# The first fp32 sums of down's adapter set one product later, and the next network's first weights scaled ahead of the low rows of t

## The chip, the cores and the metric

The kernel runs on one core of a Trainium2 chip. The metric is the time of one execution on the device, in microseconds (us); each kernel was run several times, and the median is given. Beside that there is one profiled execution of the kernel before. Its instruction records are the trace.

Five engines work side by side, each through its own list of instructions in order: TensorE (PE; its weight loads are PEld), VectorE (DVE), ScalarE (ACT), GpSimd (POOL) and SyncE (SP, which here only starts transfers). They hand work to one another by semaphores: an instruction raises a count when it is done, and another engine's list stands still at a wait until the count is reached.

## The reference, cut to what matters

The input x holds 8 samples of 128 tokens with 512 features, 1024 tokens in all. Two layers are added to it. In each, a first network is conditioned per sample by low-rank adapters that an index picks, and a feed-forward network stands behind it.

```python
# layer 0, first network (F = 1376, 16 adapters of rank 16)
gate = x @ W_gate.T + 0.5 * (x @ A_gate[id].T) @ B_gate[id].T
up   = x @ W_up.T   + 0.5 * (x @ A_up[id].T)   @ B_up[id].T
act  = silu(gate) * up
down = act @ W_down.T + 0.5 * (act @ A_down[id].T) @ B_down[id].T
# layer 0, second network (I = 1792): each weight is w * (su @ sv), rank 4
d    = silu(down @ gate_eff.T) * (down @ up_eff.T)
x    = x + d @ down_eff.T
# layer 1: a 512x512 product with bias and adapters, then a network of
# group-scaled integer weights (I = 1792)
x    = x + int_ffn(cond1(x))
```

The change touches two places in the first half: the sums `act @ A_down[id].T` (called t here) of the first network, and the step in which the first tile of the second network's weights is multiplied with its rank-4 scale.

## The kernel before

Tokens lie along the free axis, in two chunks `c` of 512; features lie on the 128 partitions. A product of fp32 accuracy is made of three passes of the PE with operands split into a high and a low part: high x high, high x low, low x high. The high part is a copy by ACT, the low part a subtraction by DVE (`lo`, line 1295). So every weight tile goes through one ACT and one DVE instruction before the PE uses it, and so does every result that is multiplied again.

The work before the integer network is a list of phases: "cond gate/up a", "cond down a", "cond gate/up b", "cond down b", "ffn0 gate/up a", and so on. A gate/up phase runs over tiles of 128 hidden features. For each tile the PE makes four products in this order (`gate_up_tile`, line 1902): gate of chunk 0, up of chunk 0, gate of chunk 1, up of chunk 1. Each is 12 matmuls and 2 adapter matmuls (line 1848). ACT then takes the silu (984), DVE multiplies with up (1395), ACT and DVE make the high and the low part (994, 1295). The first two tiles of the first phase are done together, so that all their results come at once; the third tile is the first of the ordinary kind.

The sums t of down's adapter are made along the way, in fp32, out of the fp32 product `gated`. `t_down` (2106) takes one hidden tile: 8 records of a matmul with 32 columns, summed in the bank `ps_m`, and it first waits until that tile's and its neighbour's products are made (`prod_done`) and until the adapters are in order (`a_dn_ready`). It is called for two tiles at a time, inside the third and the fifth tile of a gate/up phase, behind the gate product of chunk 0. `gated` is reused every second tile, so ACT's next silu into it waits for `t_read`, which `t_down` raises.

In "cond down b" the order around the change is written out by hand. In step o = 0 the PE makes the scale of the second network's first weight tile in the bank `ps_gates` (`scales`, 1880), half of the first down product, the last `t_down`, and the other half. DVE then masks and halves t (line 1673), makes its low part in 8 small pieces (`lo_of_t_down`, 1341), and calls `first_weights` (1537): it waits for the weights' transfer (`first_raw_in`) and for the scale (`m_ready`), multiplies the two (1542, raises `w_prod`), and goes on with three block sums and two low parts of the weights. In step o = 1 the PE starts with the scale of the second weight tile in `ps_m`. It waits for t to be masked, because that scale overwrites `ps_m`, and for `w_prod` to reach 1:

```python
if ph.name == "cond down b" and 2 * i + jj == 1:
    pe.wait_ge(t_masked, CH + 1)
    scales(following[ph], 0, 1)      # waits for w_prod >= 1
```

Behind that stand the next down product (12 to 15 matmuls a chunk) and `down_adapters` (2084), which needs the high and the low rows of t (`t_hi_rows`, `t_lo_rows_done`).

Of the kernel before, what the change touches and what calls it, by code (L numbers as in the profile page):

```python
# [61 lines left out]
def plan_phases():  # L62
    steps = [
        ("cond gate/up a", "gate_up", "cond", 0, CUT, 0, 1, "split"),
        ("cond down a", "down", "cond", 0, HK, 0, 1, "split"),
        ("cond gate/up b", "gate_up", "cond", 1, NKD - CUT, CUT, 1, "split"),
        ("cond down b", "down", "cond", 1, HK, CUT, 2, "split"),
        ("ffn0 gate/up a", "gate_up", "ffn0", 0, 7, 0, 1, "scale"),
        ("ffn0 down a", "down", "ffn0", 0, HK, 0, 1, "scale"),
        ("ffn0 gate/up b", "gate_up", "ffn0", 1, 7, 7, 1, "scale"),  # L70
        ("ffn0 down b", "down", "ffn0", 1, HK, 7, 1, "scale"),
        ("cond1", "down", "cond1", 0, HK, 0, 1, "split"),
    ]

    t0, s0, g0, d0 = 0, 0, 0, 0
    phases = []
    for name, kind, layer, part, tiles, first, loads, prep in steps:
        s0 += name == "ffn0 gate/up a"
        phases.append(Phase(name, kind, layer, part, tiles, first, t0, s0, g0, d0, loads, prep))
        t0 += tiles  # L80
        s0 += tiles
        if kind == "gate_up":
            g0 += CH * tiles
        else:
            d0 += CH * tiles
    return phases
# [78 lines left out]
def adaln_ffn(nc, d, out):  # L165
    phases = plan_phases()
# [6 lines left out]
    with ExitStack() as ctx:  # L173
# [176 lines left out]
        def chunk(c):  # L350
            return slice(c * CT, (c + 1) * CT)
# [4 lines left out]
        def widths(ph, i, jj):  # L356

            if ph.layer == "cond" and ph.part == 1 and isinstance(i, int) and 2 * i + jj == ph.tiles - 1:
                return F0_TAIL
            return P  # L360
# [11 lines left out]
        def slot(ph, jj, i):  # L372

            return (ph.s0 + jj) % 2
# [38 lines left out]
        def pair_tokens(pair):  # L413
            return slice(pair * PT, (pair + 1) * PT)
# [3 lines left out]
        def pair_sums(c):  # L418
            return slice(c * CT, c * CT + PT)
# [7 lines left out]
        def quarter(n):  # L427
            return slice(n * PR, (n + 1) * PR)
# [856 lines left out]
        def _(dve):  # L1285
# [8 lines left out]
            def lo(out_, value, hi):  # L1294
                return nc.vector.tensor_tensor(out_, value, hi.bitcast(F32), ALU.subtract)  # L1295
# [36 lines left out]
            def lo_of_t(c, nets):  # L1332
                dve.wait_ge(t_hi_done, (0 if nets == 2 else CH + 1) + c + 1)
                for g in range(nets):
                    for half in range(2):
                        rows = quarter(2 * g + half)
                        for row in (2, 3) if nets == 1 else (2,):
                            last = lo(t_rows[quarter(row), g, pair_tokens(2 * c + half)], gated[rows, c, 0:PT], t_hi[rows, c, 0:PT])
                last.then_inc(t_lo_rows_done, 1)

            def lo_of_t_down():

                dve.wait_ge(t_hi_done, CH + 1)
                for c in range(CH):
                    for pair in (2 * c, 2 * c + 1):
                        for row in (2, 3):
                            last = lo(t_rows[quarter(row), 0, pair_tokens(pair)], gated[quarter(pair), 0, 0:PT], t_hi[quarter(pair), 0, 0:PT])
                    last.then_inc(t_lo_rows_done, 1)
# [166 lines left out]
            def piece_lo(ph, j, piece):  # L1515

                q, cols = tile_of(ph, j), pieces[piece]
                if piece == 2:
                    dve.wait_ge(w_hi_done, ph.t0 + j)
                else:  # L1520
                    dve.wait_ge(piece_hi_done, 2 * q + piece + 1)
                value = w7_total[j % 2][:, cols] if piece else raw_weights(ph, j)[:, 2 * P:6 * P]
                lo(w7_lo[j % 2][:, cols], value, w7_hi[j % 2][:, cols]).then_inc(w_ready if piece == 2 else piece_ready, 1)

            def block_sums(ph, j, part):

                raw, low = raw_weights(ph, j), w7_total[j % 2]
                half = raw.rearrange("p (r h n) -> p r h n", r=2, h=2)
                if part == 0:
                    nc.vector.tensor_tensor(low[:, pieces[1]].rearrange("p (r n) -> p r n", r=2), half[:, :, 0],  # L1530
                                            half[:, 0:1, 1].to_broadcast([P, 2, 2 * P]), ALU.add).then_inc(w_summed, 1)
                elif part == 1:
                    nc.vector.tensor_tensor(low[:, 12 * P:14 * P], raw[:, 4 * P:6 * P], raw[:, 6 * P:8 * P], ALU.add).then_inc(w_summed, 1)
                else:
                    nc.vector.tensor_tensor(low[:, 8 * P:12 * P], raw[:, 0:4 * P], raw[:, 4 * P:8 * P], ALU.subtract).then_inc(w_summed, 1)

            def first_weights(ph):

                dve.wait_ge(first_raw_in, 16)
                dve.wait_ge(m_ready, 1)  # L1540
                raw = w_raw_first[:, :]
                nc.vector.tensor_tensor(raw, raw, ps_gates[:, :], ALU.mult).then_inc(w_prod, 1)
                dve.wait_ge(w_prod, 1)
                for part in range(3):
                    block_sums(ph, 0, part)
                for piece in range(2):
                    piece_lo(ph, 0, piece)
# [121 lines left out]
            def small_t(ph):  # L1669

                if ph.name == "cond down b":
                    dve.wait_ge(t_read, NKD)
                    nc.vector.scalar_tensor_tensor(out=gated[:, 0, 0:PT], in0=ps_m[:, 0:PT], scalar=0.5, in1=seg_mask[:, :],
                                                   op0=ALU.mult, op1=ALU.mult).then_inc(t_masked, 1)
                    lo_of_t_down()
                    first_weights(named["ffn0 gate/up a"])
                    return
                for c in range(CH):
                    here = gated[0:RB, c, 0:PT]
                    dve.wait_ge(t_lo_rows, c + 1)  # L1680
                    nc.vector.scalar_tensor_tensor(out=here, in0=ps_m[0:RB, pair_sums(c)], scalar=2.0, in1=here, op0=ALU.mult, op1=ALU.add).then_inc(t_added, 1)
                    dve.wait_ge(t_added, c + 1)
                    nc.vector.tensor_tensor(here, here, seg_mask[0:RB, :], ALU.mult).then_inc(t_masked, 1)
                for c in range(CH):
                    lo_of_t(c, 1)

            nc.vector.memset(warm[:, :].bitcast(F32), 0.0).then_inc(warm_zero, 1)
            for n, item in enumerate(start):
# [4 lines left out]
                else:  # L1693
                    _, c, k = item
# [13 lines left out]
            for ph in phases:  # L1708
# [33 lines left out]
                def adapters_step(ph, o):  # L1742

                    nxt = following.get(ph)
                    if o == 0:
                        tile_lo(ph, 0, 1)
                        small_t(ph)
# [82 lines left out]
        def _(pe):  # L1830
# [71 lines left out]
            def gate_up_tile(ph, i, jj):  # L1902
                s, m = slot(ph, jj, i), widths(ph, i, jj)
                pe.wait_ge(w_ready, ph.t0 + 2 * i + jj)
                for c in range(CH):
                    n = ph.g0 + CH * (2 * i + jj) + c
                    for g, (ps, read, ready) in enumerate(((ps_gate, silu_done, gate_ready), (ps_up, prod_done, up_ready))):
                        if not isinstance(i, int) or n >= CH:

                            pe.wait_ge(read, n - 3 if ph is phases[0] and 2 * i + jj == 2 else n - 1)  # L1910

                        def input_ready(k, c=c, g=g):

                            if g == 0 and ph.name == "ffn0 gate/up a" and jj == 0 and isinstance(i, int) and i == 0:
                                pe.wait_ge(h_ready, CH * k + c + 1)

                        last = sums(ps[c], m, s, g * HK * P, range(HK), lambda k, r, c=c: h_hi[0:r, k, chunk(c)],
                                    lambda k, r, c=c: h_lo[0:r, k, chunk(c)], before=input_ready, stop=ph.layer != "cond")
                        if ph.layer == "cond":
                            last = gate_up_adapters(ps[c], m, ph, 2 * i + jj, g, c)  # L1920
                        last.then_inc(ready, 1)
                        if g == 0 and c == 0 and 2 * i + jj in (2, 4):
                            for j in (2 * i + jj - 2, 2 * i + jj - 1):
                                t_down(ph, j)

# [349 lines left out]
```

## Time and profile before

| | us |
|---|---|
| median of 3 runs | 640.12 (639.88 to 640.39) |
| the profiled execution's own time | 636.58 |
| its span, first to last instruction | 635.0 |
| PE busy | 620.7 |
| DVE busy | 449.1 |
| ACT busy | 315.3 |
| POOL busy | 245.1 |

The mean granted clock of TensorE is 0.999 of full speed. A row of the page's or the trace's answers has the start, the duration, the engine, the line of the kernel, the operation with what it writes and reads, and in brackets how long the engine had been idle and who ended that. Matmuls are pipelined, so their durations overlap; what counts is when the next one starts.

### The profile page before, as it was taken

The numbers are of one execution on the slowest core, as the hardware profiler recorded it, in microseconds if no ns is written. First come the engines' busy times: TensorE is split into PE (matmuls) and PEld (weight loads), VectorE is DVE, ScalarE is ACT, GpSimd is POOL, SyncE is SP. The second block draws the span as 40 slices with busy tenths as digits, with TensorE's granted clock in tenths as the row PEclk, the third lists the DMA queues.
The fourth block names the chain that finished last, engine by engine and source line by source line (L and its number), as shares of the span: only waits on it lengthen the run. The fifth ranks groups of instructions, "written<-read, shape, count | busy, mean of one in ns | idle before, by whom it ended". The sixth has DMA issues, their size and how long they took to land.

```text
span 635.0 us, 8094 instructions
## 1 busy us (share of the span) xinstructions
PE 620.7 (98%) x2964; PEld 497.1 (78%) x2964; DVE 449.1 (71%) x540; ACT 315.3 (50%) x418; POOL 245.1 (39%) x197
## 2 busy tenths in 40 slices
PE   8989999999998999999999999999999999999996
PEld 6768788788777876778787787878787888788885
DVE  4475454544457998885437888735678998999987
ACT  5664525344634344443113444425557887478860
POOL 3670010000000006752023656440003898959986
PEclk9999999999999999999999999999999999999999
DMA  8750022101021111321102100152213211212203
GB/s 254 177 149 26 26 85 87 57 13 44 21 73 51 49 34 59 140 59 59 33 34 99 34 33 30 61 112 52 93 67 101 62 59 62 101 66 69 82 0 133
DMA packets 24474, 45.19 MB, mean 71 GB/s; under 512 B 9972, under 2 KB 12020, under 8 KB 24372
## 3 DMA queue, kind: packets, MB, share of 16 engines
q1 hardware_dynamic: 21972, 40.80, 20.9%
q0 software_dynamic: 2176, 3.36, 2.0%
q8 instruction: 24, 0.39, 0.2%
q10 hardware_dynamic: 288, 0.52, 0.2%
q14 instruction: 14, 0.11, 0.1%
HBM read 40.74 MB, written 2.10 MB: 67 GB/s over the span
## 4 chain that ended last, share of the span: by engine, by line
PE 83%; DVE 6%; ACT 3%; issue 3%; POOL 1%; SPq 1%; DMA 1%; DVEq 0%
PE ps_down L1838 7%; PE ps_down L1839 7%; PE ps_down L1840 7%; PE ps_up L1838 4%; PE ps_up L1839 4%; PE ps_up L1840 4%; PE ps_m L2020 3%; PE ps_m L2021 3%; PE ps_up L2020 3%; PE ps_gate L2020 3%; PE ps_down L2020 3%; PE ps_down L2021 3%; PE ps_gate L2021 3%; PE ps_up L2021 3%; PE ps_gate L1838 2%
## 5 line engine op out<-in xcount | busy, mean ns | idle before, releaser
L813 POOL TENSOR_TENSOR act_lo<-up,act_hi 128x512 fp32r<-128x512 f32 x14 | 18.2, 1298 | 195.7 <-ACT act_hi L1086 195.7
L1838 PE MATMUL ps_down<-act_hi,w_hi 128*128 128x512 f32 (+1 forms) x180 | 71.2, 396 | 0.0
L1839 PE MATMUL ps_down<-act_lo,w_hi 128*128 128x512 f32 (+1 forms) x180 | 70.3, 391 | 0.0
L1840 PE MATMUL ps_down<-act_hi,w_lo 128*128 128x512 f32 (+1 forms) x180 | 70.1, 389 | 0.0
L844 POOL TENSOR_TENSOR up_sum<-up_sum,up_more 128x1024 f32<-128x1024 f32 x14 | 33.7, 2410 | 64.4 <-DVE up_more L1411 64.4
L1295 DVE TENSOR_TENSOR w_lo<-w_raw,w_hi 128x512 fp32r<-128x512 f32 (+4 forms) x41 | 44.4, 1083 | 18.1 <-ACT w_hi L915 13.4
L915 ACT ACTIVATE w_hi<-w_raw 128x1024 fp32r<-128x1024 f32 (+4 forms) x30 | 27.0, 900 | 45.9 <-DVE w_raw L1302 22.0
L1838 PEld LDWEIGHTS ps_down<-act_hi,w_hi 128*128 128x128 f32 (+1 forms) x180 | 33.8, 188 | 7.8 <-issue 0.4
L1840 PEld LDWEIGHTS ps_down<-act_hi,w_lo 128*128 128x128 f32 (+1 forms) x180 | 33.8, 188 | 7.2
L1839 PEld LDWEIGHTS ps_down<-act_lo,w_hi 128*128 128x128 f32 (+1 forms) x180 | 33.8, 188 | 6.6
L1295 DVE TENSOR_TENSOR b_rows<-b_raw,b_hi 32x1024 fp32r<-32x1024 f32 (+2 forms) x23 | 25.4, 1104 | 19.2 <-ACT b_rows L933 12.0
L1411 DVE SCALAR_TENSOR_TENSOR gate_sum<-ps_up,s_group,gate_sum 128x1024 f32<-128x1024 f32 x28 | 35.8, 1280 | 4.0 <-PE ps_up L2021 4.0
L856 POOL TENSOR_TENSOR act_lo<-gate_sum,act_hi 128x1024 fp32r<-128x1024 f32 x14 | 38.3, 2747 | 0.0
L1838 PE MATMUL ps_up<-h_hi,w_hi 128*128 128x512 f32 (+1 forms) x96 | 38.0, 396 | 0.0
L1839 PE MATMUL ps_up<-h_lo,w_hi 128*128 128x512 f32 (+1 forms) x96 | 37.6, 392 | 0.0
L1840 PE MATMUL ps_up<-h_hi,w_lo 128*128 128x512 f32 (+1 forms) x96 | 37.4, 389 | 0.0
L1658 DVE TENSOR_TENSOR xp<-xp,ps_down 128x512 f32<-128x512 f32 x20 | 13.6, 684 | 31.6 <-PE ps_down L1840 30.5
L1080 ACT ACTIVATE w_hi<-w_total 128x512 fp32r<-128x512 f32 (+1 forms) x28 | 20.7, 739 | 30.6 <-POOL w_total L807 18.3
L1295 DVE TENSOR_TENSOR w_lo<-w_total,w_hi 128x512 fp32r<-128x512 f32 (+1 forms) x28 | 27.6, 986 | 10.8 <-ACT w_hi L1080 10.7
L1965 PE MATMUL ps_gate<-x_hi,w_hi 128*128 128x512 f32 x80 | 31.9, 398 | 1.0 <-ACT m_copy L1066 0.9
L1838 PE MATMUL ps_gate<-h_hi,w_hi 128*128 128x512 f32 (+1 forms) x80 | 31.6, 395 | 0.3 <-DVE h_lo L1295 0.3
L1839 PE MATMUL ps_gate<-h_lo,w_hi 128*128 128x512 f32 (+1 forms) x80 | 31.4, 392 | 0.0
(295 smaller groups left out, 1784.1 us busy)
## 6 DMA issues: line engine op xcount, KB each, us to landing
w_int<-in_ffn_gu SPq DMA_DIRECT2D x14, 512.0 KB, 3.5
w_raw<-in_cond_gu SPq DMA_DIRECT2D x9, 512.0 KB, 3.4
w_raw<-in_ffn_gu SPq DMA_DIRECT2D x9, 512.0 KB, 3.6
w_raw<-in_ffn_dn SPq DMA_DIRECT2D x8, 448.0 KB, 3.3
w_int<-in_ffn_dn SPq DMA_DIRECT2D x8, 448.0 KB, 3.2
xp<-in_x SPq DMA_DIRECT2D x8, 256.0 KB, 5.3
w_raw_third<-in_ffn_gu SPq DMA_DIRECT2D x4, 512.0 KB, 3.5
xp<-in_x SPq DMA_DIRECT2D x1, 2048.0 KB, 9.4
```

Source lines behind the costliest of these rows:

```text
L844: nc.gpsimd.tensor_tensor(up_sum[:, u % 3, :], up_sum[:, u % 3, :], up_more[:, u % 2, :], ALU.add).then_inc(up_done, 1)
L856: nc.gpsimd.tensor_tensor(act_lo[:, j, :], gate_sum[:, u % 4, :], act_hi[:, j, :].bitcast(F32), ALU.subtract).then_inc(unit_ready, 1)
L915: nc.scalar.activation(w_hi[:, s, n], w_raw[:, s, n], ACT.Copy).then_inc(w_hi_done, 1)
L1080: nc.scalar.activation(w7_hi[j % 2][:, pieces[piece]], value, ACT.Copy).then_inc(done, 1)
L1295: return nc.vector.tensor_tensor(out_, value, hi.bitcast(F32), ALU.subtract)
L1411: return nc.vector.scalar_tensor_tensor(out=here, in0=group_bank(g), scalar=group_scale(g), in1=here, op0=ALU.mult, op1=ALU.add)
L1838: nc.tensor.matmul(ps[0:m, :], w_hi[0:r, s, cols], rhs_hi(k, r), start=start and n == 0, stop=False)
L1839: nc.tensor.matmul(ps[0:m, :], w_hi[0:r, s, cols], rhs_lo(k, r), start=False, stop=False)
L1840: last = nc.tensor.matmul(ps[0:m, :], w_lo[0:r, s, cols], rhs_hi(k, r), start=False, stop=stop and n == len(ks) - 1)
L1965: nc.tensor.matmul(banks[n][:, :], w7_hi[s][:, cols], x_hi[n][:, k, :], start=not more and k == 0, stop=False, skip_group_check=more)
L2020: nc.tensor.matmul(bank[:, chunk(c)], weights, hi[:, chunk(c)], start=True, stop=False)
L2021: last = nc.tensor.matmul(bank[:, chunk(c)], weights, lo[:, chunk(c)], start=False, stop=True)
```

## The change

It does two things. In the third tile of the first phase the two calls of `t_down` move from behind the gate product of chunk 0 to behind the up product of chunk 0. In the other places (the fifth tile, and both places of "cond gate/up b") they stay. And `first_weights` is cut in two: its wait for the transfer and the scale and its product become `first_product`, which DVE calls between the masking of t and `lo_of_t_down`.

```diff
-            def first_weights(ph):
+            def first_product():
 
                 dve.wait_ge(first_raw_in, 16)
                 dve.wait_ge(m_ready, 1)
                 raw = w_raw_first[:, :]
                 nc.vector.tensor_tensor(raw, raw, ps_gates[:, :], ALU.mult).then_inc(w_prod, 1)
+
+            def first_weights(ph):
+
                 dve.wait_ge(w_prod, 1)
                 for part in range(3):
                     block_sums(ph, 0, part)
...
                     nc.vector.scalar_tensor_tensor(out=gated[:, 0, 0:PT], in0=ps_m[:, 0:PT], scalar=0.5, in1=seg_mask[:, :],
                                                    op0=ALU.mult, op1=ALU.mult).then_inc(t_masked, 1)
+                    first_product()
                     lo_of_t_down()
                     first_weights(named["ffn0 gate/up a"])
...
-                        if g == 0 and c == 0 and 2 * i + jj in (2, 4):
+                        if c == 0 and (g, 2 * i + jj) in ((int(ph is phases[0]), 2), (0, 4)):
                             for j in (2 * i + jj - 2, 2 * i + jj - 1):
                                 t_down(ph, j)
```

On the PE, in the third tile, the order before is this. `ps_gate` and `ps_up` are the gate and up sums of the chunk, `gated` and `gated_odd` the products of the first and the second tile; the 9 matmuls left out are of the same up product.

```order
L1848 MATMUL ps_gate<-t_rows,b_rows 128x256 x2
L2113 MATMUL ps_m<-gated,a_dn 32x256 x4
L2113 MATMUL ps_m<-gated_odd_58,a_dn 32x256 x4
L1838 MATMUL ps_up<-h_hi,w_hi 128x512
L1839 MATMUL ps_up<-h_lo,w_hi 128x512
...
L1848 MATMUL ps_up<-t_rows,b_rows 128x256 x2
L1838 MATMUL ps_gate<-h_hi,w_hi 128x512
```

With the change (whose lines are 4 further down in this part of the file) the same place reads:

```order
L1852 MATMUL ps_gate<-t_rows,b_rows 128x256 x2
L1842 MATMUL ps_up<-h_hi,w_hi 128x512
L1843 MATMUL ps_up<-h_lo,w_hi 128x512
...
L1852 MATMUL ps_up<-t_rows,b_rows 128x256 x2
L2117 MATMUL ps_m<-gated,a_dn 32x256 x4
L2117 MATMUL ps_m<-gated_odd_58,a_dn 32x256 x4
L1842 MATMUL ps_gate<-h_hi,w_hi 128x512
```

The two groups over `a_dn` stand behind the up product's 14 matmuls and ahead of the gate product of chunk 1.

On DVE, in step o = 0 of "cond down b", the difference is the following. `seg_mask` is the mask of t, `t_rows` the low rows of t, `w_raw_first` the second network's first weights.

```order
 L1295 TENSOR_TENSOR w_lo<-w_raw,w_hi 128x640
-L1673 SCALAR_TENSOR_TENSOR gated<-ps_m,seg_mask 128x256
+L1676 SCALAR_TENSOR_TENSOR gated<-ps_m,seg_mask 128x256
+L1542 TENSOR_TENSOR w_raw_first<-w_raw_first,ps_gate 128x1024
 L1295 TENSOR_TENSOR t_rows<-gated,t_hi 32x256 x8
-L1542 TENSOR_TENSOR w_raw_first<-w_raw_first,ps_gate 128x1024
 L1530 TENSOR_TENSOR w_total_97<-w_raw_first 128x512
 L1533 TENSOR_TENSOR w_total_97<-w_raw_first 128x256
```

The product of 1024 columns moved ahead of the eight low parts; the block sums stay behind them. ACT's and SP's lists, and POOL's, are as they were.

## Rows read from the trace of the kernel before

**Rows 1.** The page: the span, and the granted clock in 40 slices.
```profile
span 635.0 us, 8094 instructions
...
PEclk9999999999999999999999999999999999999999
```

**Rows 2.** The waits of PE over the whole span, longest first.
```profile
engine line waited for: us in total, times, longest us
PE ps_m L1880 <- DVE w_raw_first L1542: 2.2, 1, 2.2
PE ps_m L2113 <- DVE gated_odd L1395: 2.0, 1, 2.0
...
PE ps_gate L1965 <- ACT m_copy L1066: 0.9, 1, 0.9
```

**Rows 3.** Busy time of each engine in stretches, with PE's granted clock.
```profile
core 0: us, PE busy (x) PEld busy (x) DVE busy (x) ACT busy (x) POOL busy (x), PEclk, DMA share, GB/s
...
192.00:195.00 3.00, 0.81 (x10) 0.57 (x9) 2.91 (x6) 1.44 (x3) 0.00 (x0) 1.00 0.00 0
...
220.00:245.00 25.00, 24.02 (x108) 18.73 (x107) 24.14 (x39) 12.45 (x22) 4.04 (x3) 1.00 0.14 51
```

**Rows 4.** PE in order of time, third to fifth tile: start, us, line.
```profile
38.11 0.40 PE L1848 MATMUL ps_gate<-t_rows,b_rows 128*128 128x256 f32 x2
...
40.55 0.64 PE L2113 MATMUL ps_m<-gated,a_dn 128*32 128x256 f32 x8 [2.04 <-DVE gated_odd L1395]
...
41.55 0.50 PE L1838 MATMUL ps_up<-h_hi,w_hi 128*128 128x512 f32 x1
...
44.40 0.40 PE L1848 MATMUL ps_up<-t_rows,b_rows 128*128 128x256 f32 x2
...
62.51 0.40 PE L1838 MATMUL ps_gate<-h_hi,w_hi 128*128 128x512 f32 x1
```

**Rows 5.** DVE and ACT in order of time, beside the third tile.
```profile
39.73 0.67 DVE L1395 TENSOR_TENSOR gated_odd<-gated_odd,ps_m 128x512 f32<-128x512 f32 x1
...
44.30 0.60 ACT L984 ACTIVATE gated<-ps_gate 128x512 f32<-128x512 f32 x1
...
59.10 1.23 DVE L1295 TENSOR_TENSOR w_lo<-w_raw,w_hi 128x1024 fp32r<-128x1024 f32 x1
```

**Rows 6.** PE in order of time, "cond down b", from step 0 into step 1.
```profile
191.81 0.39 PE L1840 MATMUL ps_down<-act_hi,w_lo 96*128 96x512 f32 x1
...
194.39 0.66 PE L1880 MATMUL ps_m<-pack_long,pack_short 32*128 32x128 f32 x8 [2.19 <-DVE w_raw_first L1542]
...
198.53 0.63 PE L1848 MATMUL ps_down<-t_rows,b_down 128*128 128x256 f32 x4
```

**Rows 7.** DVE in order of time, "cond down b".
```profile
188.62 0.42 DVE L1673 SCALAR_TENSOR_TENSOR gated<-ps_m,seg_mask 128x256 f32<-128x256 f32 x1 [1.94 <-PE ps_m L2113]
189.53 3.46 DVE L1295 TENSOR_TENSOR t_rows<-gated,t_hi 32x256 fp32r<-32x256 f32 x8 [0.48 <-ACT t_hi L952]
193.02 1.22 DVE L1542 TENSOR_TENSOR w_raw_first<-w_raw_first,ps_gate 128x1024 f32<-128x1024 f32 x1
...
197.03 0.82 DVE L1295 TENSOR_TENSOR w_lo<-w_raw,w_hi 128x640 fp32r<-128x640 f32 x1
...
201.36 1.22 DVE L1302 TENSOR_TENSOR w_raw<-w_raw,ps_m 128x1024 f32<-128x1024 f32 x1 [1.11 <-DMA w_raw<-in_ffn_gu]
203.40 0.82 DVE L1295 TENSOR_TENSOR w_lo<-w_raw,w_hi 128x640 fp32r<-128x640 f32 x1 [0.81 <-ACT w_hi L915]
...
214.15 0.69 DVE L1658 TENSOR_TENSOR xp<-xp,ps_up 128x512 f32<-128x512 f32 x1 [0.60 <-PE ps_up L1848]
...
220.38 1.29 DVE L1295 TENSOR_TENSOR x_lo<-x_total,x_hi 128x512 fp32r<-128x512 f32 x2 [0.29 <-ACT x_hi L1061]
```

**Rows 8.** The first weights' transfer: when it was issued, and us to landing.
```profile
183.82 0.34 SPq L731 DMA_DIRECT2D w_raw_first<-in_ffn_gu  x1
...
w_raw_first<-in_ffn_gu SPq DMA_DIRECT2D x1, 512.0 KB, 3.5
```

## The prediction, made before the changed kernel ran

> **What bounds the kernel.** The views were read in this order. The page first: over a span of 635.0 us the granted clock is at its full level in every slice [rows 1]. Then PE's waits over the whole span. PE is busy nearly all the time, so an idle stretch of PE is a candidate for time that can come off the end, and only two of those waits are longer than a microsecond and a half in the middle of the kernel: 2.2 us of the scale product L1880 on DVE's product of the first weights, and 2.0 us of the fp32 sums L2113 on DVE's product of the second tile [rows 2]. The change moves one instruction group at each of them. Then the order of time around each, on the engine that waits and on those it waits for [rows 4 to 8].
>
> **First part: the fp32 sums one product later.** What is there: the two adapter matmuls of gate, chunk 0, start at 38.11 us; PE then stands for 2.04 us, until DVE's product of the second tile is done at 39.73 + 0.67 = 40.40 us, and the sums start at 40.55 [rows 4, 5]. They take until 41.55, 1.00 us, and then comes up, chunk 0, whose adapter matmuls start at 44.40; with their 0.12 us spacing the product fills 41.55 to about 44.63, 3.08 us.
> With the change, up starts right behind the gate product: 40.55 - 2.04 = 38.51 us. It ends at 38.51 + 3.08 = 41.59. The sums come next, and what they wait for has been there since 40.40, so 1.2 us of cover are left. They take their 1.00 us as before, on the path both times. Gate, chunk 1, starts at 42.6 in place of 44.6. **Term: -2.04 us.** Nothing is added and nothing else changes its place.
> What could be late next: the silu of this tile's gate, chunk 0, waits for the sums to have read the old `gated`. They end at 42.6 at the latest, and ACT comes to it only at 44.30, since it is busy with adapter pieces until then [rows 5]; 1.7 us of cover. That silu does not move with PE. PE writes its bank next in the fourth tile, three products of 3.08 us and the sums behind 38.5, at about 48.7, 3.8 us after the silu's end, so it does not hold PE either; were the cover gone, those 3.8 us would be the next. The fifth tile is the nearest thing with less room: its low weights are made at 59.10 to 60.33 and PE starts on it at 62.51 [rows 4, 5], 2.2 us of room against 2.04 gained. Even if DVE did not move at all there, PE would just not wait; and DVE and ACT are released there by results of the third tile's last product, which come 2 us earlier too.
>
> **Second part: the weights' product ahead of t's low parts.** What is there: PE's last matmul of step 0 starts at 191.81 and leaves the engine free at 192.20; the scale product starts at 194.39, 2.19 us idle. It waited for DVE, whose order was mask (188.62, 0.42), wait for ACT's high part (0.48), eight low parts (189.53, 3.46), product (193.02, 1.22, done 194.24) [rows 6, 7]. Of the 3.0 us from 192 to 195 PE was busy for 0.81 [rows 3].
> With the change the product stands behind the mask. Its operands: the scale is made in step 0, before the first down product; the transfer was issued at 183.82 and took 3.5 us, so it is there by 187.4 [rows 8], 1.6 us before DVE asks. The product runs 189.05 to 190.27 and PE, which comes at 192.20, finds it done, with 1.9 us of cover. The other condition, t masked, is met at 189.04. **Term: -2.19 us** at this place.
> What is behind the moved product on DVE: the eight low parts start at 190.27 in place of 189.53 (the 0.48 us wait for ACT now falls behind the product and is gone), and end at 193.73. PE needs them for the adapters, at 198.53 before and 198.53 - 2.19 = 196.34 now: 2.6 us of room. The block sums start at about 193.7, where they started behind 194.24; DVE is 0.5 to 0.7 us early from there on, not 2.19. This is the place where the gain can get lost.
> So I follow DVE further. Its low weights at 197.03 come some 0.6 us early; their end releases the transfer on which L1302 at 201.36 waited 1.11 us, and so that too comes 0.6 early, at 200.8, and ends at 202.0. The next low weights, at 203.40, had waited 0.81 us for ACT, and ACT for PE; with PE 2.19 us early they start when L1302 is done, at 202.0: 1.4 us early. At 214.15 DVE had waited 0.60 us for PE: it starts at 214.15 - 0.60 - 1.4 = 212.1, PE's result being there at 211.96, so 2.0 us early. At 220.38 another 0.29 us of waiting for an x part, which ACT makes behind a copy of a PE result, gives the rest: 2.2 us early [rows 7]. From 220 to 245 DVE is busy 24.14 of 25.00 us and PE 24.02 [rows 3]; PE's next wait of note, 0.9 us on `m_copy` [rows 2], lies there and hangs on DVE's chain. By then DVE is as early as PE, so it stays 0.9 and does not grow. Between 196 and 220 PE asks DVE for low weights that are made a tile ahead: those of 197.03 + 0.82 - 0.6 = 197.3 are for step 2, which PE reaches only behind the adapters of 196.3 and another half of step 1, past 200.
> The bounds of this part: 2.19 us if the above holds; 0.6 us if DVE's own lead is all that survives its busy stretch; no wait is added that could turn it below nothing unless the transfer is late (below). I take 2.1 to 2.19, since each idle stretch of DVE that makes up the lag is in the rows.
>
> **The clock.** Every slice, and the 3 us in which PE idled, has a granted clock at the 2.4 GHz level [rows 1, 3]: the two idle stretches did not lower it, so taking them away gives their own length and no more. The Trainium skill, TensorE: Matmul & The Clock Gate, section "What's actually happening", says that throttled is the default state and that activity releases it, so idle time can cost more than its length. The trace disagrees for stretches of 2 us here. It is kept as a rival, since the timed runs are longer than the profiled one.
>
> **Sum.** Span 635.0 - 2.04 - 2.19 = 630.8 us. What lies around it is 636.58 - 635.0 = 1.58, so the profiled execution would read 632.4. The median of the runs is 640.12, 3.5 us above the profiled one; I take the difference off it unchanged: 640.12 - 4.2 = **635.9 us**. A difference of 0.2% (1.3 us) is about what a measurement of this kernel can tell from no change.
>
> **Rivals.**
> *DVE keeps its lag* (0.13). The second gain shrinks because DVE is only 0.6 us early where its queue is full. Against it: DVE's waits of 0.81, 0.60 and 0.29 us on the others [rows 7]; for it: the almost full stretch behind [rows 3]. It gives 640.12 - 2.04 - 0.6 = 637.5, at the mildest 636.5.
> *One of the two waits stands up again on the spot* (0.06), on an operand I take for ready: 640.12 - 2.1 = 638.0.
> *The change does not do what it says* (0.03): both waits are only carried on to the next product, where another count is as late. 640.1. Against it: the covers of 1.2 and 1.9 us.
> *Slower* (0.03). DVE now waits for the weights' transfer with t's low parts queued behind it. If the transfer lands late, 3.46 us of low parts that used to lie beside that wait come behind it, and the block sums, the low weights and all of DVE's full stretch with them. It costs nothing until a landing at 189.0, eats up the second gain from there on, and turns to a loss once the landing is later than 193.0, 5.7 us later than seen; then DVE's chain is up to 3.46 us late: 640.12 - 2.04 + 3.46 = 641.5. For it: SP starts the next down tile's transfers right behind it; against it: 3.5 us to landing [rows 8].
> *More than the stalls* (0.05). The timed runs are 3.5 us longer than the profiled one. If that is TensorE at the 1.2 GHz level behind these two stalls, it goes with them: 640.12 - 4.2 - 3.5 = 632.4. No row shows it. By that section of the skill it could be so.
>
> **How the numbers follow.** Forecast 0.70, rivals 0.13, 0.06, 0.03, 0.03, 0.05. The range goes from the forecast with some 0.7 us of spread below, 635.2, to the case in which one half fails, 638.2; with 0.70, 0.13 and 0.06 less the edges it holds a good 8 in 10. Faster than by 1.3 us, below 638.8: 0.70 + 0.13 + 0.06 + 0.05, taken as 0.93; within: 0.04; slower: 0.03.
>
> **What would show it.** Right: PE's waits no longer have L1880 on the first weights nor the sums on `gated_odd`; the sums start near 41.6 us behind up's adapters; in "cond down b" the scale product starts near 190.2 (192.4 less the 2.04 of the first part) with no idle time ahead; the low rows of t end before PE reaches the adapters; the wait on `m_copy` is still near 0.9 us; span near 630.8. Wrong: new idle time of PE of half a microsecond or more between 194 and 245 us with DVE named, most of all a grown `m_copy` wait (DVE's lag); or idle time of DVE ahead of the product of the first weights on a transfer.

## The result: 7.4 us faster, where 4.2 were forecast

| | us |
|---|---|
| before, median of 4 runs | 640.0 (639.55 to 640.39) |
| changed, median of 4 runs | 632.55 (632.18 to 633.65) |
| ratio | 0.9887, 95% interval 0.987 to 0.9904 |
| profiled execution of before: span, granted clock | 635.0, 0.999 |
| profiled execution of the changed kernel: span, granted clock | 630.5, 1.000 |

The direction was right, and so was the span of the profiled execution (630.8 forecast, 630.5 seen). The median was not: 635.9 forecast, 632.55 measured, below the range of 635.2 to 638.2. So the two profiled executions differ by 4.5 us, about what was forecast, and the medians by 7.4. The question for the experiments is where the other 3 us were.

### The profile after

The page's first line, then PE's waits, longest first; they answer to [rows 1] and [rows 2].

```profile
span 630.5 us, 8094 instructions
```

```profile
engine line waited for: us in total, times, longest us
PE ps_m L2124 <- DVE warm L1691: 1.7, 1, 1.7
PE ps_gate L1969 <- ACT m_copy L1066: 0.9, 1, 0.9
PE ps_m L1902 <- DVE w_raw L1312: 0.7, 1, 0.7
```

Both waits of [rows 2] that the change aims at are gone, and the wait on `m_copy` is still 0.9 us. PE in order of time in the third tile, as [rows 4]: start, us, line.

```profile
37.87 0.40 PE L1852 MATMUL ps_gate<-t_rows,b_rows 128*128 128x256 f32 x2
38.10 0.40 PE L1842 MATMUL ps_up<-h_hi,w_hi 128*128 128x512 f32 x1
...
41.18 0.64 PE L2117 MATMUL ps_m<-gated,a_dn 128*32 128x256 f32 x8
...
42.18 0.50 PE L1842 MATMUL ps_gate<-h_hi,w_hi 128*128 128x512 f32 x1
```

Up follows the gate product without a gap, the sums follow up and have no idle time ahead. From the gate's adapters to the next gate product it is 42.18 - 37.87 = 4.31 us; before it was 44.63 - 38.11 = 6.5 us by [rows 4], 2.2 less. "cond down b": first DVE, as [rows 7], then PE's scale product, as [rows 6].

```profile
186.32 0.42 DVE L1676 SCALAR_TENSOR_TENSOR gated<-ps_m,seg_mask 128x256 f32<-128x256 f32 x1 [1.94 <-PE ps_m L2117]
186.66 1.21 DVE L1542 TENSOR_TENSOR w_raw_first<-w_raw_first,ps_gate 128x1024 f32<-128x1024 f32 x1
187.90 3.46 DVE L1295 TENSOR_TENSOR t_rows<-gated,t_hi 32x256 fp32r<-32x256 f32 x8
191.39 0.69 DVE L1530 TENSOR_TENSOR w_total<-w_raw_first 128x512 f32<-128x512 f32 x1
...
198.62 1.22 DVE L1302 TENSOR_TENSOR w_raw<-w_raw,ps_m 128x1024 f32<-128x1024 f32 x1 [2.47 <-DMA w_raw<-in_ffn_gu]
```

```profile
189.82 0.66 PE L1884 MATMUL ps_m<-pack_long,pack_short 32*128 32x128 f32 x8
...
193.95 0.63 PE L1852 MATMUL ps_down<-t_rows,b_down 128*128 128x256 f32 x4
```

The product is done at 187.87, 1.95 us before PE comes for it. The low rows are done at 191.36, 2.6 us ahead of the adapter matmuls. DVE waits longer for the next weights (2.47 us in place of 1.11): its additions ahead of that wait, which hang on PE's results, start at 194.88 where they started at 198.96, 4.1 us earlier, and the weights came 2.7 us earlier. No wait of PE stems from it.

### The profile page after: what moved, and what is told of

Its sections match the earlier page's. It is cut to its first block, busy times and chain, and to the rows that moved or that the text cites. A ratio compares the mean times of both kernels' runs of the same rounds, so it can differ in the third digit from the quotient of the medians.

```text
span 630.5 us, 8094 instructions
## 1 busy us (share of the span) xinstructions
PE 620.3 (98%) x2964; PEld 496.8 (79%) x2964; DVE 448.9 (71%) x540; ACT 315.3 (50%) x418; POOL 245.4 (39%) x197
## 4 chain that ended last, share of the span: by engine, by line
PE 86%; DVE 5%; ACT 3%; issue 2%; POOL 1%; DMA 1%; SPq 0%; DVEq 0%
PE ps_down L1842 7%; PE ps_down L1843 7%; PE ps_down L1844 7%; PE ps_up L1842 4%; PE ps_up L1843 4%; PE ps_up L1844 4%; PE ps_gate L1842 3%; PE ps_gate L1843 3%; PE ps_m L2024 3%; PE ps_gate L1844 3%; PE ps_m L2025 3%; PE ps_up L2024 3%; PE ps_gate L2024 3%; PE ps_down L2024 3%; PE ps_down L2025 3%; PE ps_gate L2025 3%
```

## The experiments

Each kernel was profiled once and executed several times more beside the kernel before on the same chip. For every execution the span and the mean granted clock over the span are given. That list is what settles the case, so it stands first, as a whole; the kernels in it are described below.

| kernel | executions | median span | at a mean clock of 0.998 or more: count, median span | at 0.997 or less: count, median span |
|---|---|---|---|---|
| before | 68 | 636.9 | 17, 635.2 | 51, 637.5 |
| sums moved alone | 10 | 634.6 | 4, 633.2 | 6, 635.8 |
| product moved alone | 6 | 634.5 | 2, 633.3 | 4, 635.0 |
| changed | 19 | 631.1 | 19, 631.1 | 0 |
| changed, 1 us idle added | 9 | 632.2 | 9, 632.2 | 0 |
| changed, 2 us idle added | 12 | 634.2 | 6, 633.5 | 6, 635.0 |
| changed, 5 us idle added | 12 | 637.4 | 0 | 12, 637.4 |
| sums one product later still | 5 | 630.8 | 5, 630.8 | 0 |
| and adapters ordered later | 5 | 631.2 | 5, 631.2 | 0 |

### Each half alone

The first kernel has only the condition in PE's gate/up tile from the change:

```diff
-                        if g == 0 and c == 0 and 2 * i + jj in (2, 4):
+                        if c == 0 and (g, 2 * i + jj) in ((int(ph is phases[0]), 2), (0, 4)):
```

> Only the fp32 sums of the third tile are moved; the weights' product stays behind the low rows of t. By the sum of the prediction the span falls by 2.04 us, and PE's wait of 2.2 us on the first weights stays. Theory 1 (clock): the kernel before loses 3.2 us more in its timed runs than in its profiled one because TensorE falls to its lower level behind one of the two stalls. Then the timed gain is 2.0 us, or 2.0 + 3.2 = 5.2 us if this stall is the one. Theory 2 (the extra 3.2 us has nothing to do with the stalls): the timed gain over the kernel before on the same chip is 2.0 us here, and 4.2 us, not 7.4, for the whole change when both are timed side by side.

The second has only the product:

```diff
                                                    op0=ALU.mult, op1=ALU.mult).then_inc(t_masked, 1)
+                    first_product()
                     lo_of_t_down()
```

> Only the product of the first weights is moved ahead of the low rows of t; the fp32 sums stay behind gate's chunk 0 and PE waits 2.0 us there. By the sum the span falls by 2.19 us. Theory 1 (clock): the timed gain is 2.2 us, or 2.2 + 3.2 = 5.4 us if the stall in cond down b is the one behind which the clock falls. Theory 2: 2.2 us timed.

Measured: 636.22 and 636.07 us against 638.49 for the kernel before on that chip; ratios 0.9962 (0.9947 to 0.9977) and 0.9952 (0.9936 to 0.9968). The two halves are worth about the same and add up to the whole. Theory 1 in the form in which it was put, that one of the two stalls is the one behind which the clock falls, is wrong: neither half alone brings the 5 us. But the clock is not out of it: with either half alone it is still low in most executions, 6 of 10 and 4 of 6. The profiled execution of the first one is one of these. These are PE, DVE and the others in stretches of 2 us behind the remaining stall, with the granted clock ahead of the last two columns:

```profile
core 0: us, PE busy (x) PEld busy (x) DVE busy (x) ACT busy (x) POOL busy (x), PEclk, DMA share, GB/s
190.00:192.00 2.00, 0.39 (x2) 0.00 (x0) 1.94 (x4) 0.98 (x3) 0.00 (x0) 1.00 0.00 0
192.00:194.00 2.00, 1.42 (x10) 1.28 (x11) 1.97 (x4) 1.44 (x3) 0.00 (x0) 0.82 0.00 0
194.00:196.00 2.00, 2.00 (x6) 1.52 (x6) 2.00 (x4) 0.45 (x1) 0.00 (x0) 0.50 0.00 0
196.00:198.00 2.00, 2.00 (x9) 1.59 (x8) 0.04 (x1) 0.00 (x0) 0.00 (x0) 0.83 0.40 76
```

```profile
192.58 0.66 PE L1880 MATMUL ps_m<-pack_long,pack_short 32*128 32x128 f32 x8 [2.19 <-DVE w_raw_first L1542]
...
194.55 0.63 PE L1838 MATMUL ps_up<-act_hi,w_hi 128*128 128x512 f32 x1
```

The wait is the same 2.19 us as in [rows 6]. Behind it TensorE is at 0.50 of full speed, the 1.2 GHz level, and a matmul record that takes 0.39 us elsewhere takes 0.63. What is lost is 2.0 x (0.18 + 0.50 + 0.17) = 1.7 us. The span of this execution is 634.8 us, and those of the same kernel at a clock of 0.999 are 633.1 to 634.4: 1.7 us above the shortest.

The profiled execution of the second is at a mean clock of 0.996 too, and it shows something else. PE's rows, and the clock at two places:

```profile
11.93 0.50 PE L1842 MATMUL ps_up<-h_hi,w_hi 128*128 128x512 f32 x1 [1.76 <-DVE w_lo L1295]
...
12.97 0.63 PE L1843 MATMUL ps_up<-h_lo,w_hi 128*128 128x512 f32 x1
...
44.03 0.64 PE L2117 MATMUL ps_m<-gated,a_dn 128*32 128x256 f32 x8 [2.07 <-DVE gated_odd L1395]
```

```profile
14.00:16.00 2.00, 2.00 (x7) 1.54 (x6) 0.74 (x2) 1.36 (x3) 1.79 (x5) 0.50 1.22 262
...
44.00:46.00 2.00, 1.97 (x20) 1.34 (x21) 1.27 (x2) 1.96 (x3) 0.00 (x0) 1.00 0.86 242
```

The stall that this kernel keeps, 2.07 us at the sums, did not lower the clock this time. It fell near the start of the kernel instead, behind a wait of 1.76 us for low weights whose transfer was late (ACT had waited 2.09 us for it). So a low mean clock does not prove by itself that one of the two stalls was behind it. In the other twelve traces PE's longest wait in that tile is 1.2 us, and its clock stayed full behind it. None of the 38 executions of kernels with both stalls gone (the changed one, the two with more cover, the one with 1 us added) was at 0.997 or less. So the low clock in most executions goes with the two stalls, and a fall at such a third place is rare.

### Before and changed once more

> The kernel before, timed against itself, with the granted clock and the span of each run. Theory 1 (clock): most runs read about 640 us with a granted clock visibly below that of the profiled run (0.999), and some read 636.6 with a clock near 1. Theory 2: the clock is the same in the long and the short runs, and the extra time is elsewhere. Ratio 1.000 either way, give or take 0.2%.

> The changed kernel, timed side by side with the kernel before on the same chip. Theory 1 (clock): 7.4 us less than before (ratio 0.9885), its runs at a clock of 0.998 to 1.000. Theory 2: if the two were only timed under different conditions, 4.2 us less (ratio 0.9934).

Measured: 638.51 us against 638.49, ratio 0.999 (0.9977 to 1.0004), and for the changed kernel 633.5 us, ratio 0.9912 (0.9897 to 0.9927). Theory 1 holds for the spread: the executions of before at a clock of 0.999 have spans of 634.6 to 635.6 in this run, those at 0.994 and 0.995 have 637.9 to 639.2. The gain on this chip is 5.0 us, between the two theories' numbers: the kernel before is 1.5 us lower here than in the first measurement (638.5 against 640.0) and the changed one 0.95 us higher. On the two chips of the experiments below it is 6.15 and 6.6 us, so the 7.4 us of the first measurement was not reached again. The profiled execution of before shows two things that the first profile didn't. PE's waits:

```profile
PE ps_m L2113 <- DVE gated_odd L1395: 4.0, 1, 4.0
PE ps_m L1880 <- DVE w_raw_first L1542: 2.2, 1, 2.2
```

DVE in order of time ahead of the first of them:

```profile
38.91 0.97 DVE L1359 COPY a_dn<-a_dn_raw 128x1280 f32<-128x1280 f32 x2 [1.98 <-DMA a_dn_raw<-in_a_dn_tail]
39.81 1.21 DVE L1295 TENSOR_TENSOR w_lo<-w_raw,w_hi 128x1024 fp32r<-128x1024 f32 x1
40.94 0.67 DVE L1395 TENSOR_TENSOR gated_odd<-gated_odd,ps_down 128x512 f32<-128x512 f32 x1
41.54 0.67 DVE L1395 TENSOR_TENSOR gated_odd<-gated_odd,ps_m 128x512 f32<-128x512 f32 x1
```

And the clock around it, in stretches of 2 us:

```profile
40.00:42.00 2.00, 0.00 (x0) 0.00 (x0) 2.00 (x3) 0.35 (x1) 2.00 (x5) 0.67 0.25 65
42.00:44.00 2.00, 1.64 (x16) 0.68 (x16) 1.50 (x3) 1.97 (x4) 2.00 (x5) 0.50 0.91 253
44.00:46.00 2.00, 2.00 (x8) 1.49 (x5) 0.00 (x0) 1.99 (x2) 1.75 (x4) 0.50 0.30 87
46.00:48.00 2.00, 2.00 (x7) 1.53 (x6) 1.85 (x2) 0.68 (x2) 0.00 (x0) 0.62 0.22 83
```

DVE orders down's adapters (L1359) ahead of the third tile's low weights and the second tile's products. Their transfers were late here; DVE waited 1.98 us for them, the product came at 41.54 where [rows 5] have 39.73, and PE's stall grew from 2.04 to 3.97 us. The larger part of the lateness is POOL's, which starts these transfers:

```profile
18.00 1.28 POOL L769 TENSOR_SCALAR_AFFINE_SELECT seg_mask<-seg_mask 32x256 f32<-32x256 f32 x1
...
34.75 0.52 POOL L778 DMA_DIRECT2D a_dn_raw<-in_a_dn_tail  x1
```

It started the last of them at 34.75, and in the first profile at 32.95, 1.8 us earlier. Of this 0.9 us is one mask instruction that took 1.28 us in place of 0.40. The slowest of the transfers then took 4.1 us to land, in place of 3.2.

The clock fell within this stall: from 40 to 42 us, in which PE ran nothing, it is 0.67. It was at 0.50 for the work behind: about 0.8 + 1.0 + 0.8 = 2.6 us lost, the idle part left out. The stall's 1.9 us and the clock's together are 4.5 us, a little more than the 639.2 - 635.0 = 4.2 us by which this execution is longer than the first profiled one, in which neither happened.

### An idle stretch where the change has nothing to do

Is it the idle time that lowers the clock, or something that runs at those two places? Three kernels add a wait of PE to the changed kernel in the first tile of "cond gate/up b", each for work of another engine that comes anyway. Theory A says that it is the idle time, theory B that it is the place.

```diff
                         last.then_inc(ready, 1)
+                        if (ph.name, 2 * i + jj, g, c) == ("cond gate/up b", 0, 1, 0):
+                            pe.wait_ge(prod_done, n + 1)
```

This is the first. In the second the wait is `pe.wait_ge(act_ready, n + 1)`; in the third it is `pe.wait_ge(b_hi_done, CUT + 4)`, behind chunk 1.

> The changed kernel as it is, the reference for the three idle stretches timed beside it. Both theories: every run at a clock of 0.998 to 1.000, 5 to 7 us below the kernel before, whose runs spread from 0.994 to 0.999.

> The changed kernel with one added wait: in the first tile of cond gate/up b, behind up of chunk 0, PE waits until DVE has made that product (about 1.0 us by the trace), then goes on. Theory A (any idle stretch of PE of about 2 us can lower the granted clock, in some runs, and a longer one more surely): 1.0 us more than the changed kernel, clock still 0.998 to 1.000, or lower in few runs. Theory B (the clock falls because of what runs at the two places of the change, not because PE idles): 1.0 us more, no run below 0.998.

> The same wait made longer: PE waits for the low part of that product (about 2.3 us by the trace), a place that has nothing to do with the change. Theory A: 2.3 us more than the changed kernel and in about half of the runs another 1.5 to 3 us, these runs at a clock of 0.997 or less. Theory B: 2.3 us more in every run, clock 0.998 to 1.000.

> PE waits behind up of chunk 1 of the same tile until ACT has copied the next adapter piece (about 4.9 us by the trace). Theory A: 4.9 us more and another 1.5 to 3.5 us in nearly every run, clock 0.994 to 0.996. Theory B: 4.9 us more, clock 0.998 to 1.000.

Measured: 632.67 us for the changed kernel, 633.84, 635.83 and 639.02 us with the added waits, and 638.82 for the kernel before on this chip; the ratios to it are 0.9906, 0.992, 0.996 and 1.0015, their 95% intervals 0.0024 to 0.0035 to either side. PE's added wait in the trace of each, 1 us, 2 us and 5 us:

```profile
PE ps_gate L1842 <- DVE gated L1395: 0.9, 1, 0.9
```

```profile
PE ps_gate L1842 <- DVE act_lo L1295: 2.2, 1, 2.2
```

```profile
PE ps_gate L1842 <- ACT b_rows L933: 4.7, 1, 4.7
```

Theory A holds, theory B falls. 0.9 us of idle time cost about 1.1 us of span, and the clock was never below 0.998. 2.2 us made two groups: six executions at 633.3 to 633.7, 2.4 us above the changed kernel's median of 631.1, and six at a clock of 0.993 to 0.997 with spans of 634.7 to 638.5, with a median another 1.5 us up. Behind 4.7 us every one of twelve executions was at a clock of 0.996 or less, and the cost was 6.3 us. The profiled execution of the third shows it behind the stall:

```profile
130.00:136.00 6.00, 1.38 (x8) 0.98 (x6) 1.38 (x2) 3.74 (x4) 0.00 (x0) 1.00 0.00 0
136.00:138.00 2.00, 1.91 (x5) 1.48 (x6) 1.89 (x2) 1.10 (x2) 0.00 (x0) 0.64 0.00 0
138.00:140.00 2.00, 2.00 (x6) 1.59 (x5) 1.77 (x2) 0.00 (x0) 0.00 (x0) 0.51 0.00 0
140.00:142.00 2.00, 2.00 (x11) 1.65 (x11) 0.00 (x0) 0.60 (x1) 0.00 (x0) 1.00 0.30 61
```

The clock was still full through the stall, which ended at 136.09, and fell half a microsecond after PE had gone on.

The control had its own finding: in its profiled execution the transfer of the adapters was late again, and the changed kernel waited after all. PE's row, and DVE's:

```profile
42.21 0.64 PE L2117 MATMUL ps_m<-gated,a_dn 128*32 128x256 f32 x8 [1.04 <-DVE gated_odd L1395]
```

```profile
38.78 0.96 DVE L1359 COPY a_dn<-a_dn_raw 128x1280 f32<-128x1280 f32 x2 [1.99 <-DMA a_dn_raw<-in_a_dn_tail]
```

With such a late transfer PE waited 3.97 us in the kernel before and 1.04 us in the changed one, and behind the 1.04 us the clock did not fall: 0.999 for this execution.

### More cover for the sums

The last kernels try to take this 1.04 us too.

```diff
-                        if c == 0 and (g, 2 * i + jj) in ((int(ph is phases[0]), 2), (0, 4)):
+                        if g == 0 and (c, 2 * i + jj) in ((int(ph is phases[0]), 2), (0, 4)):
```

The other one has this as well, and DVE's ordering of the adapters moved:

```diff
                 def between_tiles(ph, j):
 
+                    if ph is phases[0] and j == 1:
+                        order_a_dn()
                     p = next_piece(ph, j)
...
-                    if ph is phases[0] and j == 0:
-                        order_a_dn()
```

> The changed kernel as it is, timed beside the two below. Both theories: 5 to 7 us below the kernel before. In executions in which DVE waits about 2 us for the transfer of down's adapters, PE still waits up to 1 us for the product of the second tile ahead of the moved sums; in the others it does not.

> As the changed kernel, but the sums of the first two tiles stand behind gate of chunk 1 in the third tile, one product later again; nothing else. Theory C (the late transfer of down's adapters uses up the 1.2 us of cover that the changed kernel has): no wait of PE on the sums in any execution, 0 to 1.0 us less than the changed kernel by the execution, 0.3 to 0.5 us in the median. Rival (the wait just moves on, to ACT's silu that needs the sums' read): the same time as the changed kernel or 0.5 us more, with PE waiting for gated in the fourth tile.

> As the one before, and DVE puts down's adapters in order behind the second tile's low parts, no longer ahead of the third's low weights and the second's products. The late transfer then holds nothing that is queued behind it but adapter pieces. Theory C: DVE no longer waits for it at all (it lands some 2 us before), and the time is that of the one before, within 0.3 us: one product of cover is enough. Rival: moving DVE's wait costs where the copy (0.96 us) now stands, ahead of the low parts of the adapter piece of the fourth tile, 0 to 0.5 us more.

Measured: 632.3, 632.5 and 632.85 us, ratios to the kernel before 0.9894, 0.99 and 0.9906, each give or take 0.0025. That does not tell them apart. The part of the rival that is seen is that ACT's silu now waits for the sums, 0.95 us in the first and 1.50 in the second, without PE waiting for it:

```profile
45.36 0.60 ACT L984 ACTIVATE gated<-ps_gate 128x512 f32<-128x512 f32 x1 [0.95 <-PE ps_m L2117]
```

None of the three profiled executions had a wait of PE on the sums, and none had DVE waiting for the transfer. In the first two POOL had started it at the usual time, so they don't put theory C to the test. In the third it was late. POOL's row, and DVE's:

```profile
35.57 0.52 POOL L778 DMA_DIRECT2D a_dn_raw<-in_a_dn_tail  x1
```

```profile
41.68 1.00 DVE L1359 COPY a_dn<-a_dn_raw 128x1280 f32<-128x1280 f32 x2
```

That is later than in the two executions in which DVE waited 2 us (34.75 and 34.52), and here, with the copy behind the second tile's low parts, it did not wait at all. This is what theory C expects of the later ordering, in one execution. Whether DVE would have waited in the old order can't be read from it, and nothing came off the time. A late transfer was seen in 2 of the 12 profiled executions whose DVE rows had it ahead of the products, so 5 executions of a kernel are too few to show a gain of at most 1 us in some of them. Whether more cover is worth any time stays open. No version here beats the changed kernel.

## Why the prediction was wrong, point by point

**What bounds the kernel, and the two terms: right for the execution they were read from.** 17 executions of before at a clock of 0.998 or more have a median span of 635.2, and the 19 of the changed kernel 631.1: 4.1 us, where 2.04 + 2.19 = 4.2 were forecast. The two halves alone, at the same clock, give 635.2 - 633.2 = 2.0 and 635.2 - 633.3 = 1.9.

**The covers: right, but for one.** The weights' product had 1.95 us (1.9 forecast), the low rows of t 2.6 us (2.6 forecast). The sums' 1.2 us were 1.1 in the first profile of the changed kernel (the product was done at 40.08, the sums start at 41.18) and gone in another, since DVE's products hang on a transfer that I took for landed. The idle time of DVE in [rows 7] did make up its lag: the wait on `m_copy` stayed at 0.9 us, and the rival of DVE's lag can be left.

**The clock: this is the step that failed.** "Taking them away gives their own length and no more" rested on one execution with a clock of 0.999. In the later executions of before such a clock came in 17 of 68. In the other 51 the clock had fallen to 0.997 or less, and they are 637.5 - 635.2 = 2.3 us longer at the median; by an estimate from their mean clocks, 0.9957 against 0.999, 0.0033 x 637 = 2.1 us of this is the clock. The changed kernel was at 0.998 or more in 19 of 19. So over all executions the spans differ by 636.9 - 631.1 = 5.8 us, 1.7 us more than at a full clock. The Trainium skill, TensorE: Matmul & The Clock Gate, section "What's actually happening", was in the prediction as the rule that speaks for a larger gain, with the remark that the trace disagrees for stretches of 2 us. The trace only showed that it need not happen in every execution. The added idle time of 2.2 us, at a place that the change does not touch, did it in 6 of 12, and so the runs agree with the page that idleness throttles.

**The difference taken off the median unchanged: the same error in its arithmetic form.** The 3.5 us by which the median of before exceeded the profiled execution were not a constant around the span. The time is the span and 1.5 to 1.8 us in every execution for which both were recorded, so those runs had spans of about 638.4 us. That they were this long by the low clock and by the late transfer at the first stall is inferred from the later executions: the granted clocks of those runs were not recorded, and how their 3.2 us split between the two is not known. The one traced execution of before that has both shows 1.9 us from the transfer and 2.3 to 2.6 from the clock. The rival "more than the stalls" had this mechanism and was given 0.05. That its 632.4 lies so close to the 632.55 measured is in part luck: it stands for a gain of 7.7 us, and the three later comparisons gave 5.0 to 6.6.

**Slower, one wait left over, no effect: not seen.** The transfer of the second network's first weights never held DVE in a trace here.

## What to carry to other kernels

A profile is one execution; when the median of the runs lies 3 us above the profiled one, that difference is a term of the sum, and a stall that can lower TensorE's clock is its first suspect. The added waits give an estimate for one place of this kernel: a stall of 2.2 us cost its length and about 0.8 us more on average (1.5 us in 6 of 12), one of 4.7 us 1.6 us more, and one of 0.9 us about its length. Where an instruction that the path needs is queued behind a wait for a transfer, give its consumer cover for the transfer's spread and not for the landing seen once.

## What the runs showed of the hardware that had not been expected

- An idle stretch of TensorE of 2.2 us in the middle of steady work is followed by the 1.2 GHz level in some executions of the same program and not in others: 6 of 12 with the one added stretch. With 0.9 us it was none of 9, with 4.7 us all of 12. The kernel before, with its two stretches, had a low mean clock in 51 of 68. Near the start of the kernel one stretch of 1.76 us was enough.
- The fall costs after the stall, not in it: 1.7 us in the trace of the sums alone, 2.6 us behind the stall of 3.97 us. Matmul records of 0.39 us take 0.63 us there. Behind the stalls of 1.76, 2.19 and 4.71 us the clock was still full when TensorE went on, and fell 0.5 to 1 us later; only in the one of 3.97 us did it fall within the stall.
- With nothing changed in the kernel, POOL started the last of the 16 small adapter transfers between 32.4 and 33.2 us in ten traces and at 34.5, 34.75 and 35.6 us in three. In just these three, the last of its mask instructions ahead took 1.28 us, and in the other ten 0.40 or 0.41.
